# Part of the first expert moved into the first layer's steps, and second-layer rounds of seven chunks instead of eight

## The chip, the cores and the metric

The kernel runs on one core of one Trainium2 chip. The metric is the device time of one execution in microseconds (us). Three executions of the kernel before took 1352.67, 1353.41 and 1355.34 us; the median is 1353.41 us.

## The reference

Two transformer layers over x of shape (8, 512, 128). In each layer attention and feed-forward part read the same normalized input, and both are added to x.

```python
x = L0_attn_encodings                      # (8, 512, 128)
xn = _layernorm(x)                         # eps 1e-5
x = x + _L0_attn_ref(xn, ...) + _L0_ffn_ref(xn, ...)
xn = _layernorm(x)
x = x + _L1_attn_ref(xn, ...) + _L1_ffn_ref(xn, ...)
# attention in both layers: 16 heads of 8, causal softmax over 512 keys
# layer 0 feed-forward: block-quantized linear 128->512, gelu, block-quantized linear 512->128
def expert_step(acc, w):                   # layer 1 feed-forward: all 8 experts for all rows
    wg, wu, wd = w                         # (128,512) (128,512) (512,128)
    h = jax.nn.silu(x @ wg) * (x @ wu)
    return (acc + h @ wd, None)
```

## The kernel before, in words

There are three parts in a row, each a block of its own with a barrier behind it: `layer0`, `attend_moe` (the second layer) and `finish`. Every engine's program is written out in a fixed order; engines meet only at semaphores. No scheduler decides anything.

**First layer.** Attention goes by quads: four heads of one batch, 32 quads in all. One step g of `layer0` computes the row maxima of quad g+1 (scores, six units S0 to S5), the exponentials of half of quad g-1 and half of quad g (transposed scores, units T), the product with the values for quad g-1 (PV), and the feed-forward part of one 128-row tile of layer 0 (q = g-1). u = g mod 4 says which of the batch-wise jobs a step also holds: projections, transposes and the late copies of a batch. Steps run from -7 to 32. The order on TensorE in a step is: scores_and_keys 0, a batch job, fillers 1, scores_and_keys 1, a batch job, fillers 2, scores_and_keys 2, fillers 3, scores_and_keys 3, fillers 4, scores_and_keys 4, PV, scores_and_keys 5, and the end of the step. A filler (`keep_warm`, one 128x128 by 128x512 matmul into `pv_bank`, whose result nobody reads) only occupies TensorE; the table FILLERS says how many stand at each of the four places: 8, 14, 11 and 9 in steps with u = 0, 1, 2, 3.

Matmul results of the first layer live in three pairs of PSUM banks that are used in turn. `units_in_order` lists every unit in program order; unit number i uses pair i mod 3, and `begin` makes TensorE wait until unit i-3 has been read out (`read_out` names the semaphore). So whichever engine reads unit i-3 late holds up unit i, and everything behind it on TensorE.

VectorE reads the score units (`maxima_of`), and between unit 1 and unit 2 it computes the quantization scales of the feed-forward tile (`magic_tile`: a reduce of 512 columns and two small instructions).

**Second layer.** `attend_moe` interleaves attention with the experts. One chunk is 128 of the 512 hidden columns of one expert for one batch: TensorE does `gate_up` (6 matmuls of 512 columns, since every operand is a high and a low part and three products are needed), ScalarE tanh, VectorE `silu` and `product`, ScalarE `hi`, GpSimd `lo`, and TensorE three chunks later `down` (3 matmuls). Every fourth chunk VectorE adds the result to `acc`. There are 8 experts x 8 batches x 4 = 256 chunks, 8 in each of 32 quads. Score units stand in chunks 0 to 5 of a quad, key units in chunks 1 to 6, the transposed maxima (`maxima_rows`, which wait for GpSimd's `rest_of_maxima`) in chunk 7. `LATE` names what is left over from the first layer or is due in a quad (the projections of batches 6 and 7, the attention's share of a batch).

**Hand-over.** The first layer's last step (32) holds only keys, PV and one tile; behind them VectorE takes the statistics of batch 6 and GpSimd normalizes it, and then the second block starts.

## Time and profile before

| | |
|---|---|
| time, median of three | 1353.41 us |
| the profiled execution | 1358.98 us, of which 1357.2 us are the span of the trace |
| mean granted TensorE clock | 0.975 of 2.4 GHz |
| TensorE matmul / weight load busy | 1289.3 us (95%) / 773.8 us (57%) |
| VectorE / ScalarE / GpSimd busy | 980.6 (72%) / 824.3 (61%) / 744.0 us (55%) |
| fillers (L148) | 402 matmuls |
| steps 10 to 29 of the first layer | 182.5 to 475.3 us |
| second layer | 516.6 to about 1333 us |

An engine's busy time counts an instruction from its start to its end; matmuls overlap, so that their pace is read from the distance of two starts. "Idle before" gives an engine's wait and the instruction whose end released it. In rows, L134 are scores, L141 keys (transposed scores), L148 fillers, L159 PV, L950 the mask, L702 and L169 the row maxima, L1562 to L1564 gate and up, L1573 to L1575 down, L1522 the transposed maxima.

### The profile page before, as it was taken

Reading aid. Unit: us, or ns where it says so; the run is one execution under the profiler, and the core shown is the slowest. Engines: PE = TensorE matmul, PEld = TensorE weight load, DVE = VectorE, ACT = ScalarE, POOL = GpSimd, SP = SyncE. Lnnn points to the kernel's source line nnn. Section 1 sums busy time; section 2 is a strip of 40 time slices with the busy share of each in tenths; the row PEclk is TensorE's granted clock in tenths of the full one; section 3 lists DMA queues with packets and bytes.
Section 4 is the critical chain, followed back from the end, with each engine's and each line's share of the span. In section 5 each row is a group of like instructions: output and inputs, shape, how many; then the busy total and the mean of one; then the engine's idle time right before and its main releaser. Section 6 shows DMA issues by size and latency. Waiting matters only on the chain. (4 is left out here: it accounts for less than half of the span.)

```text
span 1357.2 us, 23492 instructions
## 1 busy us (share of the span) xinstructions
PE 1289.3 (95%) x8320; PEld 773.8 (57%) x8328; DVE 980.6 (72%) x2338; ACT 824.3 (61%) x1235; POOL 744.0 (55%) x890
## 2 busy tenths in 40 slices
PE   7899999999999987999999999999999999999996
PEld 5444545554454444656666666666666666666664
DVE  4676777777776666777777777777787788787764
ACT  2456676666765654666566666566566566566561
POOL 6154465655655444665655655655655655655551
PEclk9899999999998897999999999999999999999998
DMA  6222233324433230111211211111111110101002
GB/s 189 67 86 79 88 116 104 123 93 138 128 102 110 72 104 28 42 43 61 66 43 52 73 44 37 42 43 38 42 44 37 41 51 31 42 28 30 18 16 86
DMA packets 57682, 90.93 MB, mean 67 GB/s; under 512 B 12087, under 2 KB 23356, under 8 KB 57566
## 3 DMA queue, kind: packets, MB, share of 16 engines
q1 hardware_dynamic: 56414, 88.91, 21.0%
q8 instruction: 67, 1.10, 0.3%
q10 hardware_dynamic: 1152, 0.52, 0.2%
q14 instruction: 49, 0.40, 0.1%
HBM read 43.75 MB, written 44.53 MB: 65 GB/s over the span
## 5 line engine op out<-in xcount | busy, mean ns | idle before, releaser
L1262 POOL TENSOR_TENSOR a_h_lo<-a_h,a_h_hi 128x512 fp32r<-128x512 f32 x256 | 328.7, 1284 | 139.1 <-ACT a_h_hi L1341 135.8
L193 POOL TENSOR_SCALAR_AFFINE_SELECT E<-E 128x256 f32<-128x256 f32 (+1 forms) x384 | 194.6, 509 | 346.4 <-ACT E L1349 199.4
L702 DVE TENSOR_REDUCE mx<-bank_pair 128x2 f32<-128x1024 f32 (+3 forms) x264 | 209.5, 818 | 117.5 <-PE bank_pair L950 116.2
L1422 DVE SCALAR_TENSOR_TENSOR a_h<-a_h,bank_pair 128x512 f32<-128x512 f32 x256 | 175.5, 686 | 164.1 <-ACT a_h L1337 164.0
L1349 ACT ACTIVATE E<-bank_pair 128x1024 f32<-128x1024 f32 (+1 forms) x192 | 169.6, 883 | 105.2 <-PE bank_pair L141 105.0
L169 DVE CUSTOM_DVE_ANT_0 bank_pair<-bank_pair,mask 128x512 f32<-128x512 f32 x496 | 230.3, 516 | 0.0
L1341 ACT ACTIVATE a_h_hi<-a_h 128x512 fp32r<-128x512 f32 x256 | 161.6, 631 | 110.8 <-DVE a_h L1428 110.8
L134 PE MATMUL bank_pair<-st 24*128 24x512 f32 (+3 forms) x1024 | 201.6, 390 | 21.0 <-DVE mx L169 8.4
L790 ACT ACTIVATE E<-bank_pair 128x1024 f32<-128x1024 f32 (+1 forms) x192 | 168.3, 878 | 69.7 <-PE bank_pair L141 68.1
L1337 ACT ACTIVATE a_h<-bank_pair 128x512 f32<-128x512 f32 x256 | 151.3, 591 | 77.7 <-PE bank_pair L1564 75.4
L1428 DVE TENSOR_TENSOR a_h<-a_h,bank 128x512 f32<-128x512 f32 x256 | 175.9, 687 | 26.7
L141 PE MATMUL bank_pair<-st 26*128 26x512 f32 (+3 forms) x1024 | 185.2, 392 | 2.0 <-DVE mx L702 1.4
L134 PEld LDWEIGHTS bank_pair<-st 24*128 24x128 f32 x1024 | 99.0, 185 | 115.4 <-issue 72.3
L148 PE MATMUL bank<-identr 128*128 128x512 f32 x402 | 139.5, 461 | 2.0 <-POOL identb L492 2.0
L141 PEld LDWEIGHTS bank_pair<-st 26*128 26x128 f32 x1024 | 88.4, 184 | 69.1 <-issue 55.4
L159 PE MATMUL bank<-E,V 128*9 128x512 f32 (+3 forms) x1024 | 86.2, 456 | 3.5 <-POOL E L193 3.5
L148 PEld LDWEIGHTS bank<-identr 128*128 128x128 f32 x402 | 73.9, 206 | 20.0 <-issue 10.1
L159 PE MATMUL bank_pair<-E,V 128*9 128x512 f32 (+3 forms) x1024 | 80.7, 434 | 0.0
L169 DVE DVE_READ_ACCUMULATOR2_ANT mx<- 128x1 f32 x496 | 69.6, 140 | 0.0
L950 PE MATMUL bank_pair<-mask,identb 128*128 128x128 bf16 (+1 forms) x396 | 65.4, 248 | 0.0
L1573 PE MATMUL bank<-a_h_hi,a_w_hi 128*128 128x512 f32 x128 | 63.7, 498 | 1.6 <-POOL a_h_lo L1262 1.6
L1573 PE MATMUL bank<-a_h_hi,w_hi 128*128 128x512 f32 x128 | 64.2, 501 | 0.0
(203 smaller groups left out, 2294.7 us busy)
## 6 DMA issues: line engine op xcount, KB each, us to landing
st<-stack_d SPq DMA_DIRECT2D x256, 96.0 KB
o_d<-O SPq DMA_DIRECT2D x64, 256.0 KB, 2.1
stack_d<-l_q_k_hi SPq DMA_DIRECT2D x56, 256.0 KB, 3.2
stack_d<-l_q_k_lo SPq DMA_DIRECT2D x28, 256.0 KB, 3.4
st<-ms SPq DMA_DIRECT2D x128, 8.0 KB
wst<-wg_in SPq DMA_DIRECT2D x8, 256.0 KB, 3.2
wst<-wu_in SPq DMA_DIRECT2D x8, 256.0 KB, 3.1
wst<-wd_in SPq DMA_DIRECT2D x8, 256.0 KB, 3.6
```

The source lines that it names most:

```text
L134: return nc.tensor.matmul(bank[:, col:col + w], st[rows, 0, bass.ts(t, P)], st[rows, 1, 0:w], start=first, stop=last)
L141: return nc.tensor.matmul(bank[:, col:col + w], st[rows, 1, bass.ts(kb, P)], st[rows, 0, N - w:N], start=True, stop=True)
L148: nc.tensor.matmul(bank[:, :], identr[:, :], columns, start=True, stop=True)
L159: ins = nc.tensor.matmul(pv_bank[VW * c:VW * c + HD + 1, N - w:N], V[:, v:v + HD + 1], E[:, (PLANES * g + j) % slots, at:at + w], start=kb ...
L169: ins = nc.vector.tensor_tensor_reduce(part, part, mask[:, N - w:N], 1.0, NEG, ALU.add, ALU.max, mx[:, g % 2, NT - 1 - kb, PLANES * r + j: ...
L193: return nc.gpsimd.affine_select(out=part, in_=part, compare_op=ALU.is_ge, fill=0.0, base=0, pattern=pattern, channel_multiplier=-1)
L702: ins = nc.vector.tensor_reduce(out, pair[:, :, col:col + width(kb)], AX.X, ALU.max)
L790: nc.scalar.activation(E[:, pair % SLOTS_E, at_col:at_col + HALVES * w].rearrange("p (r c) -> p r c", r=HALVES), pair_of("T", g, n)[:, :, ...
L1262: nc.gpsimd.tensor_tensor(h_lo[:, q % RH, :], h[:, q % RH, :], h_hi[:, q % RH, :].bitcast(F32), ALU.subtract).then_inc(h_lo_ready, 1)
L1349: nc.scalar.activation(E[:, pair % SLOTS_E, at_col:at_col + HALVES * w].rearrange("p (r c) -> p r c", r=HALVES), T_banks[:, :, 0:w], ACT.E ...
L1422: nc.vector.scalar_tensor_tensor(hq, hq, 1.0, g_bank[:, :], ALU.add, ALU.mult).then_inc(silu_ready, 1)
L1428: nc.vector.tensor_tensor(hq, hq, u_bank[:, :], ALU.mult).then_inc(h_ready, 1)
```

## The change

- The first 20 chunks of expert 0 (batches 0 to 4) are computed in steps 10 to 29 of the first layer, one chunk e = g - 10 a step. In each of them stand three groups of three matmuls: `gate` behind filler place 1, into `pv_bank`; `down` of the chunk before (e-1), unit D, ahead of scores_and_keys 2; `up`, unit U, ahead of scores_and_keys 3. D and U take their turn in the three bank pairs.
- In these steps EARLY_FILLERS replaces FILLERS: 2, 7, 2 and 2 fillers for u = 0 to 3.
- ScalarE gets `tanh` (ahead of exp 4 of quad g-1) and `high` (behind exp 0 of quad g); VectorE `silu` and `add_down` behind `magic_tile` and ahead of the maxima of unit 2, and `product` behind them; GpSimd `low` behind the first causal of quad g. `add_down` adds four chunks into `acc_early` and is what frees unit D.
- Expert 0 is loaded at step 4 and split at steps 6 to 8 (before: loaded at 22, split at 24 to 28); expert 1 is loaded at step 31.
- The second layer has 236 chunks. Quads 0 to 11 keep 8 chunks, quads 12 to 31 have 7. `PASSES` gives the order of (expert, batch). In a quad of seven, key unit 5, the transposed maxima and what follows them share the last chunk, and `rest_of_maxima` stands in chunk 5.
- `outputs(g-1)`, the copy of PV's result, moves from chunk 3 to the last chunk of the quad, ahead of `hi`; the store of it moves to the end of SyncE's round. A late unit of attention comes one quad later.
- Layer end (step 32): GpSimd's last causal goes ahead of the tile's shift, ten fillers stand ahead of the last PV, VectorE's statistics of batch 6 stand earlier, and the normalization of batch 6 moves into the second layer's quad 0 (GpSimd, chunk 3).
- `bv` is one row instead of four, `at` is multiplied in place, and `st_rows` shares its buffer with `h`.

The first place is VectorE in step 12 (u = 0) of the first layer, from maxima of unit 1 on. In rows `bank_pair` is a unit, L702 or L761 its maxima, l_gelu the tile. Before:

```order
L702 TENSOR_REDUCE mx<-bank_pair 128x2 x2
L612 TENSOR_REDUCE l_amax<-l_gelu 128x16
L614 TENSOR_SCALAR l_amax<-l_amax 128x16
L616 TENSOR_SCALAR l_magic<-l_amax 128x16
L702 TENSOR_REDUCE mx<-bank_pair 128x2 x2
L619 TENSOR_TENSOR l_quant<-l_shifted,l_magic 128x512
L702 TENSOR_REDUCE mx<-bank_pair 128x2 x3
```

Now (L776 silu, L790 add_down, L781 product):

```order
L761 TENSOR_REDUCE mx<-bank_pair 128x2 x2
L671 TENSOR_REDUCE l_amax<-l_gelu 128x16
L673 TENSOR_SCALAR l_amax<-l_amax 128x16
L675 TENSOR_SCALAR l_magic<-l_amax 128x16
L776 SCALAR_TENSOR_TENSOR l_h<-l_h,bank 128x512
L790 SCALAR_TENSOR_TENSOR acc_early<-bank_pair,acc_early 128x512
L761 TENSOR_REDUCE mx<-bank_pair 128x2
L781 TENSOR_TENSOR l_h<-l_h,bank_pair 128x512
L761 TENSOR_REDUCE mx<-bank_pair 128x2
L678 TENSOR_TENSOR l_quant<-l_shifted,l_magic 128x512
L761 TENSOR_REDUCE mx<-bank_pair 128x2 x3
```

Two instructions now stand between the tile's scales and the maxima of unit 2, and a third behind these.

The second place is TensorE in the same step, from the end of scores_and_keys 1 to fillers 4. Before:

```order
L148 MATMUL bank<-identr 128x512 x2
L141 MATMUL bank_pair<-st 128x256 x2
L134 MATMUL bank_pair<-st 128x256 x2
L950 MATMUL bank_pair<-mask,identb 128x128 x2
L148 MATMUL bank<-identr 128x512 x2
L141 MATMUL bank_pair<-st 128x512 x2
L134 MATMUL bank_pair<-st 128x512 x2
L950 MATMUL bank_pair<-mask,identb 128x128 x2
L148 MATMUL bank<-identr 128x512 x2
```

Now, from unit D on (L1070 to L1072 are down and then up, L170 scores, L177 keys, L184 fillers):

```order
L1070 MATMUL bank_pair<-l_h_hi,w_hi 128x512
L1071 MATMUL bank_pair<-l_h_hi,w_lo 128x512
L1072 MATMUL bank_pair<-l_h_lo,w_hi 128x512
L177 MATMUL bank_pair<-st 128x256 x2
L170 MATMUL bank_pair<-st 128x256 x2
L1049 MATMUL bank_pair<-mask,identb 128x128 x2
L1070 MATMUL bank_pair<-xT_hi,w_hi 128x512
L1071 MATMUL bank_pair<-xT_hi,w_lo 128x512
L1072 MATMUL bank_pair<-xT_lo,w_hi 128x512
L177 MATMUL bank_pair<-st 128x512 x2
L170 MATMUL bank_pair<-st 128x512 x2
L1049 MATMUL bank_pair<-mask,identb 128x128 x2
```

Fillers 2 and 3 are gone, and the matmuls of D and of U stand in their places; fillers 4, behind the last row, stay.

The third place is TensorE at the end of a second-layer quad: the last key unit, down, gate_up and the transposed maxima. Before:

```order
L141 MATMUL bank_pair<-st 128x256 x2
L1573 MATMUL bank<-a_h_hi,a_w_hi 128x512
L1574 MATMUL bank<-a_h_hi,a_w_lo 128x512
L1575 MATMUL bank<-a_h_lo,a_w_hi 128x512
L1562 MATMUL bank_pair<-xT_hi,a_w_hi 128x512
L1563 MATMUL bank_pair<-xT_hi,a_w_lo 128x512
L1564 MATMUL bank_pair<-xT_lo,a_w_hi 128x512
L1562 MATMUL bank<-xT_hi,a_w_hi 128x512
L1563 MATMUL bank<-xT_hi,a_w_lo 128x512
L1564 MATMUL bank<-xT_lo,a_w_hi 128x512
L1522 MATMUL bank_pair<-identr,nm 8x128 x4
```

Now, in a quad of seven chunks (L1653 are the transposed maxima, L177 the last key unit, L1706 on down):

```order
L1693 MATMUL bank_pair<-xT_hi,a_w_hi 128x512
L1694 MATMUL bank_pair<-xT_hi,a_w_lo 128x512
L1695 MATMUL bank_pair<-xT_lo,a_w_hi 128x512
L1693 MATMUL bank<-xT_hi,a_w_hi 128x512
L1694 MATMUL bank<-xT_hi,a_w_lo 128x512
L1695 MATMUL bank<-xT_lo,a_w_hi 128x512
L1653 MATMUL bank_pair<-identr,nm 8x128 x4
L177 MATMUL bank_pair<-st 128x256 x2
L1706 MATMUL bank<-a_h_hi,a_w_hi 128x512
L1707 MATMUL bank<-a_h_hi,a_w_lo 128x512
L1708 MATMUL bank<-a_h_lo,a_w_hi 128x512
```

The last key unit stood one whole chunk ahead of the transposed maxima, and now follows them.

The diff, cut to its core:

```diff
-SPLIT_AT = (24, 26, 28)
+SPLIT_AT = (6, 7, 8)
+EARLY, EARLY_STEP = 5, 10
+EARLY_CHUNKS = EARLY * NC
+EARLY_FILLERS = ((0, 0, 0, 2), (6, 0, 0, 1), (0, 0, 0, 2), (0, 0, 0, 2))
+CHUNKS_OF = [8] * 12 + [7] * 20
+PASSES = [(0, 5)] + [(1, b) for b in range(5)] + [(0, 6), (0, 7)] + [(1, b) for b in range(5, B)] + [(x, b) for x in range(2, EXPERTS) for b in range(B)]
...
 # units_in_order
+        put(("D", g - EARLY_STEP - 1, 0), 0 <= g - EARLY_STEP - 1 < EARLY_CHUNKS)
         scores_and_keys(2)
         put(("X", 0, b + 2), u == 2 and 0 <= b + 2 < B)
+        put(("U", g - EARLY_STEP, 0), 0 <= g - EARLY_STEP < EARLY_CHUNKS)
         scores_and_keys(3)
...
 # read_out
+            return {"F": (gelu_ready, NT * i + 2), "U": (early_h, i + 1), "D": (early_added, i + 1),
...
 # GpSimd, first layer
+            def low(e):
+                pool.wait_ge(early_hi, e + 1)
+                nc.gpsimd.tensor_tensor(h_lo, h, h_hi.bitcast(F32), ALU.subtract).then_inc(early_lo, 1)
...
-                if q is not None:
+                if q is not None and g < QUADS:
                     shift_tile(q)
                 if in_range(g - 1):
                     causal(g - 1, 5)
+                if g == QUADS:
+                    shift_tile(q)
...
-                if u == 0 and ok(y2):
+                if u == 0 and ok(y2) and g < QUADS:
                     normalize(1, y2)
...
 # VectorE, first layer
+            def silu(e):
+                dve.wait_ge(early_tanh, e + 1)
+                nc.vector.scalar_tensor_tensor(h, h, 1.0, pv_bank[:, :], ALU.add, ALU.mult).then_inc(early_silu, 1)
+            def product(e):
+                dve.wait_ge(early_up, e + 1)
+                dve.wait_ge(early_silu, e + 1)
+                nc.vector.tensor_tensor(h, h, bank_of("U", e, 0), ALU.mult).then_inc(early_h, 1)
+            def add_down(e):
+                dve.wait_ge(early_down, e + 1)
+                ...
+                    nc.vector.scalar_tensor_tensor(a, bank_of("D", e, 0), 0.5, a, ALU.mult, ALU.add).then_inc(early_added, 1)
...
                 if q is not None:
                     magic_tile(q)
+                if g == QUADS:
+                    statistics(1, y2)
                 if u == 3 and ok(a):
                     unshift_x(a)
+                if early(g - EARLY_STEP):
+                    silu(g - EARLY_STEP)
+                if early(g - EARLY_STEP - 1):
+                    add_down(g - EARLY_STEP - 1)
                 if S:
                     maxima_of(g + 1, 2)
...
 # TensorE, first layer
+            def down(e):
+                pe.wait_ge(early_lo, e + 1)
+                begin("D", e, 0)
+                thrice(bank_of("D", e, 0), 2, e, h_hi, h_lo, True, True).then_inc(early_down, 1)
...
+                if g == QUADS:
+                    pe.wait_ge(O_copied, g - 1)
+                    keep_warm(nc, pv_bank, identr, 10)
+                if early(g - EARLY_STEP):
+                    up(g - EARLY_STEP)
                 fill(g, 3)
                 scores_and_keys(g, 3)
...
 # second layer, GpSimd and ScalarE
+            for g, c, last, q in chunks_in_order():
+                if c == CHUNKS_OF[g] - 2 and g + 1 < QUADS:
+                    rest_of_maxima(g + 1)
+                if 0 < c <= UNITS_A_QUAD:
+                    causal(g, c - 1)
+                lo(q)
...
+                tanh(q)
+                if last and g + 1 < QUADS:
+                    copy_mrow(g + 1)
+                if 0 < c <= UNITS_A_QUAD:
+                    exp(g, c - 1)
+                if last and g > 0:
+                    outputs(g - 1)
+                hi(q)
```

## Rows read from the trace of the kernel before

**Rows 1.** Windows: us, busy us (x) per engine, clock, DMA share, GB/s; stages.

```profile
182.50:240.00 57.50, 54.80 (x453) 28.61 (x454) 42.38 (x85) 38.95 (x56) 33.98 (x45) 1.00 0.37 113
851.30:1102.70 251.40, 248.37 (x1425) 158.97 (x1425) 196.97 (x518) 158.89 (x246) 148.69 (x163) 1.00 0.14 43
```

**Rows 2.** Timeline of step 12: start us, us, engine, line, op [idle before].

```profile
213.99 1.29 DVE L702 TENSOR_REDUCE mx<-bank_pair 128x2 f32<-128x768 f32 x2 [0.54 <-PE bank_pair L950]
...
216.34 1.81 DVE L702 TENSOR_REDUCE mx<-bank_pair 128x2 f32<-128x512 f32 x2
...
215.14 0.71 PE L148 MATMUL bank<-identr 128*128 128x512 f32 x2
...
215.78 0.50 PE L141 MATMUL bank_pair<-st 26*128 26x512 f32 x2
```

**Rows 3.** Timeline of steps 13 (two rows), 14 (three) and 15 (two).

```profile
229.20 1.29 DVE L702 TENSOR_REDUCE mx<-bank_pair 128x2 f32<-128x768 f32 x2 [2.46 <-PE bank_pair L950]
...
231.68 0.49 PE L141 MATMUL bank_pair<-st 26*128 26x512 f32 x2
...
243.10 1.29 DVE L702 TENSOR_REDUCE mx<-bank_pair 128x2 f32<-128x768 f32 x2 [0.92 <-PE bank_pair L950]
...
246.76 0.68 DVE L702 TENSOR_REDUCE mx<-bank_pair 128x2 f32<-128x512 f32 x1
...
247.50 0.50 PE L134 MATMUL bank_pair<-st 24*128 24x512 f32 x2 [0.54 <-DVE mx L702]
...
257.51 1.29 DVE L702 TENSOR_REDUCE mx<-bank_pair 128x2 f32<-128x768 f32 x2 [0.92 <-PE bank_pair L950]
...
260.16 0.50 PE L141 MATMUL bank_pair<-st 26*128 26x512 f32 x2
```

**Rows 4.** Timeline, VectorE in the second layer, two instructions back to back.

```profile
1088.78 0.69 DVE L1428 TENSOR_TENSOR a_h<-a_h,bank 128x512 f32<-128x512 f32 x1
1089.40 0.69 DVE L1437 SCALAR_TENSOR_TENSOR acc<-bank,acc 128x512 f32<-128x512 f32 x1
```

**Rows 5.** Timeline, last two chunks of a second-layer quad.

```profile
1099.22 0.17 DVE L1417 TENSOR_REDUCE nm<-mx 128x16 fp32r<-128x16 f32 x1
...
1099.76 0.39 PE L141 MATMUL bank_pair<-st 26*128 26x256 f32 x2
...
1100.07 0.50 PE L1573 MATMUL bank<-a_h_hi,a_w_hi 128*128 128x512 f32 x1
...
1102.27 0.40 PE L1522 MATMUL bank_pair<-identr,nm 128*8 128x128 f32 x4
```

**Rows 6.** Timeline, end of the first layer to the second layer's first matmul.

```profile
503.57 1.05 POOL L509 TENSOR_TENSOR l_shifted<-l_gelu,l_magic 128x512 f32<-128x512 f32 x1
...
505.05 3.11 PE L159 MATMUL bank<-E,V 128*9 128x512 f32 x16 [3.52 <-POOL E L193]
...
510.08 0.29 DVE L686 TENSOR_TENSOR xs<-bank,xs 128x128 f32<-128x128 f32 x1 [4.54 <-PE bank L1065]
...
513.11 3.13 POOL L504 TENSOR_SCALAR xn<-xs,mv,rstd 128x128 f32<-128x128 f32 x4
...
516.59 0.77 PE L1562 MATMUL bank_pair<-xT_hi,w_hi 128*128 128x512 f32 x1 [6.55 <-PEq L291]
```

**Rows 7.** Windows: the second layer's first 5 us.

```profile
516.00:521.00 5.00, 4.41 (x10) 2.87 (x11) 2.02 (x5) 1.21 (x2) 0.24 (x1) 0.50 0.49 146
```

**Rows 8.** Timeline, two TensorE waits of 2 us in the first layer.

```profile
73.88 0.66 PE L993 MATMUL bank_pair<-ident,l_xn 128*128 128x128 f32 x4 [2.15 <-POOL l_xn L504]
...
130.93 0.66 PE L993 MATMUL bank_pair<-ident,l_xn 128*128 128x128 f32 x4 [2.08 <-POOL l_xn L504]
```

**Rows 9.** Windows: behind either wait of rows 8, and one step at a fallen clock.

```profile
73.00:78.00 5.00, 4.12 (x20) 2.80 (x21) 1.30 (x3) 1.62 (x3) 3.18 (x6) 0.66 0.16 50
130.00:135.00 5.00, 4.07 (x35) 2.58 (x39) 2.90 (x6) 2.49 (x4) 3.66 (x7) 1.00 0.35 99
282.91:298.48 15.57, 14.61 (x108) 8.14 (x106) 10.65 (x23) 10.07 (x16) 9.56 (x13) 0.90 0.20 63
```

More of the change, by code:

```diff
@@ L236, in __init__, with acc_of @@
         self.xn, self.xnT = sb("xn1", [P, NT, D]), sb("xnT1", [P, N])
+def acc_of(acc, b):
+    return acc[0][:, bass.ts(b, N)] if b < EARLY else acc[1][:, bass.ts(b - EARLY, N)]
 def load_expert(sp, wst, experts, x, done):
@@ L587, in _ @@
                         causal(g, n)
-                if u == 0 and ok(y2):
+                        if n == 0 and early(g - EARLY_STEP):
+                            low(g - EARLY_STEP)
+                if u == 0 and ok(y2) and g < QUADS:
                     normalize(1, y2)
@@ L871, in _ @@
                     parts(0, a, 0)
+                if early(g - EARLY_STEP):
+                    tanh(g - EARLY_STEP)
                 if in_range(g - 1):
@@ L1090, in _ @@
                 fill(g, 1)
+                if early(g - EARLY_STEP):
+                    gate(g - EARLY_STEP)
                 scores_and_keys(g, 1)
@@ L1097, in _ @@
                     keys(0, a)
+                if early(g - EARLY_STEP - 1):
+                    down(g - EARLY_STEP - 1)
                 fill(g, 2)
@@ L1577, in down @@
                     ins.then_inc(acc_ready, 1)
-            for i in range(STEPS):
-                g, odd = i // PLANES, i % PLANES
-                more, back = g + 1 < QUADS, not odd and g > 0
-                for n in range(NC):
-                    gate_up(i, n)
-                    if odd and n == 3 and more:
-                        maxima_rows(g + 1)
-                        if g in LATE:
-                            late_unit(*LATE[g])
-                    c = NC * odd + n
-                    scores_and_keys(g, c if c < UNITS_A_QUAD else None, c - 1 if 0 < c <= UNITS_A_QUAD else None)
-                    if back and n == 0:
-                        PV(g - 1, 0)
-                        PV(g - 1, 1)
-                    if back and n == 1:
-                        PV(g - 1, 2)
-                        PV(g - 1, 3)
-                    if NC * i + n >= LAG:
-                        down(NC * i + n - LAG)
-            for q in range(NC * STEPS - LAG, NC * STEPS):
+            for g, c, last, q in chunks_in_order():
+                more, back = g + 1 < QUADS, g > 0
+                gate_up(q)
+                if last and more:
+                    maxima_rows(g + 1)
+                    if g in LATE:
+                        late_unit(*LATE[g])
+                scores_and_keys(g, c if c < UNITS_A_QUAD else None, c - 1 if 0 < c <= UNITS_A_QUAD else None)
+                if back and c == 0:
+                    PV(g - 1, 0)
+                    PV(g - 1, 1)
+                if back and c == 1:
+                    PV(g - 1, 2)
+                    PV(g - 1, 3)
+                if q >= LAG:
+                    down(q - LAG)
+            for q in range(NC * len(PASSES) - LAG, NC * len(PASSES)):
                 down(q)
@@ L1657, in sums @@
                     o = sum_banks[b % 4][:, bass.ts(t, D)]
-                    ins = nc.tensor.matmul(o, acc[:, bass.ds(b * N + t * P, P)], ident[:, :], start=True, stop=b < last)
+                    ins = nc.tensor.matmul(o, acc_of(acc, b)[:, bass.ts(t, P)], ident[:, :], start=True, stop=b < last)
                     if b == last:
```

279 lines of the change are left out of this document (162 added, 117 removed).

## The prediction

> **What bounds the kernel now.** I read the windows by stage first, then the timeline of single steps on TensorE and VectorE side by side, then the waits. The windows say that TensorE is busy nearly all the time in both layers: 54.8 of 57.5 us over four first-layer steps, 248.4 of 251.4 us in the second layer [rows 1]. In the first layer part of that is fillers, 8 to 14 matmuls a step. VectorE has 42.4 of 57.5 us there, and 197.0 of 251.4 in the second layer. So in the second layer real work on TensorE sets the time, and a chunk taken away is time gained. In the first layer the question is not how much room TensorE has, since fillers can go, but whether the new work waits for something that fillers never waited for. The timeline answers that.
>
> **Second layer, 20 chunks fewer.** In the last two chunks of a quad, down of one chunk starts at 1100.07 and the transposed maxima behind the next gate_up at 1102.27: nine matmuls in 2.20 us, 0.244 each [rows 5]. Chunk 7 holds nothing else that is paid by the quad, so 20 x 2.20 = 44.0 us go. What is late next: VectorE's top maxima are read at 1099.22 and end 0.17 later; with GpSimd's small instruction behind them they are ready near 1099.7, and gate_up of chunk 6 ends where the key unit starts, at 1099.76 [rows 5]. So the transposed maxima would just not wait. But with seven chunks a quad, VectorE's add into acc (0.62 from start to start, [rows 4]) moves through the quad, and in most quads it falls on a chunk with maxima, on which the next score unit or the transposed maxima wait. One add each for ten of the 20 quads is 6 us; nothing and twice that are the bounds. The output copy moves ahead of hi on ScalarE, with the store and the load of the maxima queued behind it on SyncE; down is three chunks behind, and the loaded maxima are wanted only by the first key unit of the next quad, so I take nothing for it; a load that comes late would cost up to 1 us a quad. Together -38 us (-44 to -24).
>
> **First layer, 20 steps with early work.** By instructions this is cheap. Per batch there are 36 matmuls more and 29 fillers fewer (42 against 13), 7 x 0.244 = 1.7 us, 8.5 us for five batches. But unit U takes the bank pair that unit D had, so up waits until add_down has read D. On VectorE add_down stands behind maxima 1, the tile's scales and silu, and none of these can start before scores 1 are there. In step 12 maxima 1 starts at 213.99 and the instruction behind the scales at 216.34: 2.35 us. Silu and add_down are instructions of 512 columns with a PSUM operand, 0.62 us each from start to start [rows 4], 0.1 for the semaphore (estimate), and then up, three matmuls: two fillers take 0.64 (215.14 to 215.78, [rows 2]), three 0.88. From maxima 1 to the start of scores_and_keys 3 that is 2.35 + 1.24 + 0.10 + 0.88 = 4.57 us. Before it is 215.78 - 213.99 = 1.79. The step grows by 2.8, and by another 0.24 because gate has one matmul more than the two fillers of place 1: 3.0 us (u = 0). The waits stand in front of work that is all TensorE's own, so nothing later gives them back: scores and keys 4 follow exp 0, which follows key unit 0.
>
> The other steps in the same way [rows 3]. u = 1: before 231.68 - 229.20 = 2.48, now 4.57: 2.1 us (gate and fillers 1 together are one matmul fewer there, which the transposes behind them wait for anyway). u = 2: the scales take longer, 243.10 to 246.76 is 3.66; add_down ends at 248.1, four transposes and up bring scores 3 to 249.35, against 247.50, where it already waited for VectorE: 1.85 + 0.24 = 2.1 us. u = 3: another instruction of 512 columns (unshift_x) stands ahead of silu, so 4.57 + 0.62 = 5.2 against 260.16 - 257.51 = 2.65: 2.5 us, the matmul of gate and one filler fewer at place 4 cancelling. Sum 9.7 a batch, 48.5 for five; the first early step has no unit D, -2.0. So +46.5 us. The bounds: 8.5 where the wait is hidden, and 60 where every step also pays 0.6 us for tanh ahead of exp 4, on which D waits. ScalarE's table need not change for tanh beside exp, since the second layer already runs both.
>
> **Clock.** These are waits of 1 to 2.7 us in each of 19 steps. Two waits of 2.15 and 2.08 us stand in the trace [rows 8]: behind the first the granted clock is 0.66 over 5 us, behind the second it stays at 1.00 [rows 9]; the fillers that stood there go. A step with a fall took 15.57 us [rows 9] against 57.50 / 4 = 14.4, 1.2 us more. Ten such falls are 12 us; against them stand this one and, as an estimate, two more like it that steps 10 to 29 have already, 4 us. +8 us; the bounds are -4 (no fall at all) and +34 (2 us in each of 19 steps, less the 4).
>
> **Hand-over.** The first layer's last instruction is GpSimd's normalization, from 513.11 for 3.13 us, and TensorE starts at 516.59, 0.35 behind it [rows 6]. The normalization moves; the last is then VectorE's add, 510.08 + 0.29. The tile's shift (1.05) no longer stands ahead of the last causal, and PV, 3.11 us at half clock, should take half of that behind ten fillers that fill its wait of 3.52 [rows 6]: 510.37 - 1.05 - 1.5 + 0.35 = 508.2, so -8.4 us. The second layer's first 5 us ran at clock 0.50 [rows 7]; at full clock they are worth 2.5. The normalization (4.2 us with its power) and three splits of 1.28 are then on GpSimd in quad 0, which costs 1. Sum -10 (-6 to -12).
>
> **Sum.** -38 + 46.5 + 8 - 10 = +6.5 us. The profiled execution took 1358.98 us with a span of 1357.2; it becomes 1365.5. The median of the runs shown is 5.6 below the profiled one, so 1353.4 + 6.5 = 1360 us.
>
> The other steps (6 to 8 with the splits, 30 with its unit D) I put at nothing: ScalarE and GpSimd have a third of the step free in them, and D costs 0.9 us once.
>
> **Rivals.**
> - Waits paid, nothing else. The chain D to U costs its 46.5 us, but the clock stays up, and VectorE's add finds room in the shorter quads: 1353.4 - 44 + 46.5 - 10 = 1346 us. For it: the second wait of rows 8 leaves no trace on the clock. Against it: the first one does.
> - The early work hides. Place: up in the first layer. If add_down ended before TensorE is through scores and keys 2, the early work would cost its 7 matmuls a batch alone: 1353.4 + 8.5 - 38 - 10 = 1314 us, the side away from my forecast. It decides 1.4 us behind the start of maxima 1, where up could start (215.14 - 213.99 before, and a matmul of 0.24 more, [rows 2]); add_down ends at 2.35 + 1.24 = 3.6. For it speaks the first layer's VectorE, idle for 15 of 57.5 us; against it, that this idle time lies before maxima 1, where VectorE waits for scores (0.54 to 2.46 us, [rows 2, 3]). The Trainium skill (Perfetto Trace Analysis, Identifying the Most-Contended Engine) says to judge TensorE by the busy share of its weight loads and not by that of its matmuls, and under Optimization Strategy that regimes with different bounds may gain by interleaving. Here the loads take 28.6 of 57.5 us in the first layer and 159.0 of 251.4 in the second [rows 1], which by that rule is room in the first, and the time would be that of this rival.
> - The clock falls in most early steps: +34 in place of +8 would be 1386; with some of it behind waits, 1380 us. For it: TensorE loses the fillers just where it now waits. Against it: the new matmuls are as long as fillers were.
> - The change doesn't do what it says. The order of the instructions shows D, U and 20 rounds of seven in their places, so I give it nothing.
>
> **Chances.** Forecast 0.48, with a range of its own of 1352 to 1369; waits paid alone 0.21; hidden 0.12; clock mostly low 0.19. For 8 in 10 the range takes in the first of the rivals and the last, and leaves the hidden case out: 1336 to 1384 us. A measurement of this kernel tells 0.2% (2.7 us) from no change. Faster are the two rivals below and a little of the forecast: 0.36. Within 0.2%: 0.10. Slower: 0.54.
>
> **What would show it.** Steps 10 to 29 take about 292.8 us before; with me 340 to 355, with the hidden case 300. Up (unit U) has an idle time of about 2 us in u = 0, 1 in u = 1 and 1 to 2 in u = 3, and the transposes ahead of it 2 to 3 in u = 2, all ended by VectorE's add into acc_early. The second layer's quads of seven take 22.9 us where VectorE keeps up, 23.2 with its adds. The second layer's first matmul comes 8 to 9 us sooner after the last transposed maxima of the first. If up never waits for VectorE, my largest term is wrong, and if the quads of seven are above 24 us, something other than TensorE sets them.

## The result: slower, 1386.96 us

The kernel after takes 1386.96 us (1381.84 to 1389.24, four runs), the kernel before 1353.04 us in the runs beside it: the ratio is 1.0244, 95% interval 1.0208 to 1.028. The forecast was 1360 us with 1336 to 1384 as its range, so the direction was right and the size was not: 34 us slower, where 6.5 were expected. The profiled execution took 1389.24 us, with a span of 1387.5. The profiled pair differs by less, 30.3 us of span, since the profiled execution of the kernel before was 5.6 us over its median.

The profile after, first its page: part 1 (busy us, share, instructions) and two lines of part 2 (40 slices; `PEclk` is the granted clock in tenths).

```profile
PE 1296.5 (93%) x8185; PEld 765.8 (55%) x8193; DVE 982.2 (71%) x2353; ACT 818.6 (59%) x1235; POOL 740.9 (53%) x890
...
PEclk9899988988887897999999999999999999999999
```

TensorE is busy a little longer than before (1289.3 us) though it has 135 matmuls fewer (8320 before). The second line says why: in the slices that hold steps 10 to 29 the clock is 0.7 to 0.9. The windows say it by stage: three of six pieces of steps 10 to 29, the end of the first layer, and the second layer's rounds 1 to 11 and then 19 rounds of seven. Columns as in [rows 1], which the first row answers.

```profile
181.90:240.00 58.10, 51.90 (x355) 25.73 (x357) 36.82 (x70) 32.79 (x50) 29.20 (x37) 0.82 0.31 95
...
300.00:360.00 60.00, 52.80 (x352) 25.30 (x354) 38.88 (x80) 34.97 (x52) 33.83 (x43) 0.84 0.27 81
...
420.00:486.00 66.00, 59.85 (x405) 27.65 (x405) 39.29 (x77) 35.50 (x53) 31.30 (x41) 0.80 0.22 68
...
558.00:586.00 28.00, 27.19 (x232) 15.19 (x231) 21.17 (x40) 17.26 (x25) 12.14 (x18) 1.00 0.47 144
615.30:896.60 281.30, 277.97 (x1597) 180.44 (x1596) 217.10 (x577) 182.56 (x286) 173.31 (x189) 1.00 0.16 51
896.60:1337.20 440.60, 429.44 (x2521) 274.19 (x2521) 346.83 (x941) 275.70 (x427) 245.19 (x280) 1.00 0.13 40
```

Before, the first stage had a clock of 1.00 [rows 1]. Cutting the record into windows of 2 us shows each fall: in steps 10 to 29 there are 18 falls to half clock (1.2 of 2.4 GHz) with 125.9 us spent there, against 3 and 20.4 before. A step with a fall takes 17.5 to 20.5 us; the only two without one took 16.0 (step 14) and 14.8 (step 26). In the second layer the clock is up (1.00 in both windows above).

Stage by stage, from the copies of the transposed maxima (one a step or round):

| | before | after | difference | forecast |
|---|---|---|---|---|
| steps 10 to 29 | 292.8 | 376.5 | +83.7 | +54.5 |
| last copy of layer 1 to first of layer 2 | 40.9 | 30.9 | -10.0 | -10 |
| rounds 1 to 11 | 284.3 | 281.3 | -3.0 | } -38 |
| 19 rounds from the twelfth on | 477.2 | 440.6 | -36.7 | } |

The twentieth round of seven lies behind the last copy. From there to the last down it is 27.4 us before and 26.0 after, and to the end of the span 54.2 and 50.3.

Two of the three places came out near the forecast, and so did the waits in the third. The timeline of TensorE after in steps 12 to 15 (start us, us, engine, line, operation, idle before and releaser) has L1070 as the first matmul of up and L1121 as the transposes ahead of it in u = 2:

```profile
225.59 0.50 PE L1070 MATMUL bank_pair<-xT_hi,w_hi 128*128 128x512 f32 x1 [1.74 <-DVE acc_early L790]
...
246.30 0.50 PE L1070 MATMUL bank_pair<-xT_hi,w_hi 128*128 128x512 f32 x1 [0.89 <-DVE acc_early L790]
...
266.02 0.63 PE L1121 MATMUL bank_pair<-ident,l_xn 128*128 128x128 f32 x4 [1.93 <-DVE acc_early L790]
...
281.79 0.54 PE L1070 MATMUL bank_pair<-xT_hi,w_hi 128*128 128x512 f32 x1 [1.29 <-DVE acc_early L787]
```

The forecast named about 2, 1, 2 to 3 and 1 to 2 us (u = 0, 1, 2, 3), all ended by VectorE's add into `acc_early`, as they are. The groups of steps 10 to 29 on TensorE (count, busy, mean ns, idle before by releaser) give the sum for up, 20.8 us in 20 steps:

```profile
L1070 PE MATMUL bank_pair<-xT_hi,w_hi 128*128 128x512 f32 x20 | 12.6, 630 | 20.8 <-DVE acc_early L790 13.9 <-DVE acc_early L787 6.9
```

The hand-over after, in the timeline of three engines, answers [rows 6]:

```profile
585.05 0.86 DVE L707 BATCH_NORM_STATS2 stats<-xs 128x6 f32<-128x128 f32 x4
...
587.80 1.05 POOL L562 TENSOR_TENSOR l_shifted<-l_gelu,l_magic 128x512 f32<-128x512 f32 x1
...
587.88 1.69 PE L195 MATMUL bank<-E,V 128*9 128x512 f32 x16
...
592.25 0.47 PE L1693 MATMUL bank_pair<-xT_hi,w_hi 128*128 128x512 f32 x1 [0.66 <-PEq L334]
```

PV no longer waits and runs at full clock (1.69 us for 3.11), and the second layer's first matmul waits 0.66 us, not 6.55. It comes 8.2 us sooner behind the last transposed maxima of the first layer, where 8 to 9 were forecast. Two more windows answer [rows 9] and [rows 7], a stretch of 16 us with falls (0.90 in the step there) and 5 us from the second layer's first matmul on (0.50 there):

```profile
281.00:297.00 16.00, 14.94 (x111) 7.81 (x111) 9.10 (x16) 6.83 (x10) 6.80 (x9) 0.79 0.31 93
592.00:597.00 5.00, 4.48 (x20) 2.68 (x20) 2.69 (x6) 2.23 (x4) 0.94 (x1) 1.00 0.54 162
```

### The profile page after: what moved, and what is told of

Read it like the earlier page. It is cut to its first block and busy times, and to the rows that moved or that the text cites. A ratio compares the mean times of both kernels' runs of the same rounds, so it can differ in the third digit from the quotient of the medians.

```text
span 1387.5 us, 23344 instructions
## 1 busy us (share of the span) xinstructions
PE 1296.5 (93%) x8185; PEld 765.8 (55%) x8193; DVE 982.2 (71%) x2353; ACT 818.6 (59%) x1235; POOL 740.9 (53%) x890
## 5 line engine op out<-in xcount | busy, mean ns | idle before, releaser
L1398 POOL TENSOR_TENSOR a_h_lo<-a_h,a_h_hi 128x512 fp32r<-128x512 f32 x236 | 303.1, 1284 | 105.3 <-ACT a_h_hi L1477 101.2
L761 DVE TENSOR_REDUCE mx<-bank_pair 128x2 f32<-128x1024 f32 (+3 forms) x264 | 209.9, 819 | 154.5 <-PE bank_pair L1049 154.2
L1552 DVE SCALAR_TENSOR_TENSOR a_h<-a_h,bank_pair 128x512 f32<-128x512 f32 x236 | 161.8, 686 | 134.5 <-ACT a_h L1473 133.9
L170 PE MATMUL bank_pair<-st 24*128 24x512 f32 (+3 forms) x1024 | 210.3, 407 | 19.1 <-DVE mx L205 6.1
L177 PE MATMUL bank_pair<-st 26*128 26x512 f32 (+3 forms) x1024 | 191.7, 408 | 4.8 <-DVE mx L761 3.1
L1477 ACT ACTIVATE a_h_hi<-a_h 128x512 fp32r<-128x512 f32 x236 | 148.6, 630 | 72.9 <-DVE a_h L1558 72.8
L1558 DVE TENSOR_TENSOR a_h<-a_h,bank 128x512 f32<-128x512 f32 x236 | 162.1, 687 | 26.4 <-DVE a_h L1552 2.3
L1473 ACT ACTIVATE a_h<-bank_pair 128x512 f32<-128x512 f32 x236 | 140.1, 594 | 68.3 <-PE bank_pair L1695 66.3
L170 PEld LDWEIGHTS bank_pair<-st 24*128 24x128 f32 x1024 | 104.0, 195 | 112.7 <-issue 77.3
L177 PEld LDWEIGHTS bank_pair<-st 26*128 26x128 f32 x1024 | 92.9, 193 | 74.3 <-issue 59.1
L195 PE MATMUL bank<-E,V 128*9 128x512 f32 (+3 forms) x1024 | 102.8, 527 | 0.0
L184 PE MATMUL bank<-identr 128*128 128x512 f32 x267 | 95.4, 478 | 2.0 <-POOL identb L545 2.0
L1706 PE MATMUL bank<-a_h_hi,a_w_hi 128*128 128x512 f32 x128 | 64.1, 501 | 1.3 <-POOL a_h_lo L1398 1.3
L935 ACT ACTIVATE l_hqT<-bank 128x512 bf16<-128x512 bf16 x32 | 19.1, 597 | 76.9 <-PE bank L1146 76.9
L184 PEld LDWEIGHTS bank<-identr 128*128 128x128 f32 x267 | 52.3, 217 | 12.1 <-issue 3.7
```

The costliest lines, as they stand in the source:

```text
L170: return nc.tensor.matmul(bank[:, col:col + w], st[rows, 0, bass.ts(t, P)], st[rows, 1, 0:w], start=first, stop=last)
L177: return nc.tensor.matmul(bank[:, col:col + w], st[rows, 1, bass.ts(kb, P)], st[rows, 0, N - w:N], start=True, stop=True)
L195: ins = nc.tensor.matmul(pv_bank[VW * c:VW * c + HD + 1, N - w:N], V[:, v:v + HD + 1], E[:, (PLANES * g + j) % slots, at:at + w], start=kb ...
L761: ins = nc.vector.tensor_reduce(out, pair[:, :, col:col + width(kb)], AX.X, ALU.max)
L1398: nc.gpsimd.tensor_tensor(h_lo[:, q % RH, :], h[:, q % RH, :], h_hi[:, q % RH, :].bitcast(F32), ALU.subtract).then_inc(h_lo_ready, 1)
L1477: nc.scalar.activation(h_hi[:, q % RH, :], h[:, q % RH, :], ACT.Copy).then_inc(h_hi_ready, 1)
```

## Experiments

In all of them "steps" are steps 10 to 29 of the first layer. Each was timed in turns with the kernel before.

| run | edit | time, us | ratio to before (95%) | steps, us | falls, us at half clock |
|---|---|---|---|---|---|
| 1 | scales behind the experts' work | 1354.99 | 1.0014 (0.9992 to 1.0035) | 341.0 | 8, 27.0 |
| 2 | fillers in the wait | 1348.07 | 0.9965 (0.9942 to 0.9988) | 334.5 | 2, 10.1 |
| 3 | kernel before, few fillers | 1376.63 | 1.0165 (1.0131 to 1.0199) | 314.2 | 19, 94.8 |
| 4 | fillers ahead of the wait | 1392.70 | 1.0283 (1.0222 to 1.0343) | 377.1 | 16, 88.4 |
| 5 | 1, and the last causal first | 1338.32 | 0.9896 (0.9869 to 0.9923) | 320.7 | 1, 3.4 |
| 6 | 5, and more fillers | 1344.48 | 0.994 (0.9916 to 0.9964) | 328.5 | 1, 3.4 |
| 7 | after, add to acc later | 1371.09 | 1.0145 (1.0119 to 1.0172) | 362.5 | 16, 92.0 |
| 8 | after, normalization back | 1388.07 | 1.0248 (1.0204 to 1.0292) | 366.3 | 16, 98.4 |
| 9 | 5 and 7 | 1321.37 | 0.9766 (0.9737 to 0.9795) | 322.3 | 1, 10.2 |
| 10 | 9 without fillers in the steps | 1336.88 | 0.9882 (0.9848 to 0.9915) | 328.9 | 11, 44.1 |
| 11 | 9, product behind the scales | **1315.38** | 0.972 (0.969 to 0.9749) | 314.8 | 2, 6.6 |
| 12 | kernel before, add to acc later | 1347.73 | 0.9959 (0.9944 to 0.9973) | 286.5 | 1, 3.4 |

The two right columns are of the one profiled execution each.

### 1. The wait taken away: VectorE's order

```diff
+                if early(g - EARLY_STEP - 1):
+                    add_down(g - EARLY_STEP - 1)
+                if early(g - EARLY_STEP):
+                    silu(g - EARLY_STEP)
+                    maxima_of(g + 1, 2)
+                    product(g - EARLY_STEP)
                 if q is not None:
                     magic_tile(q)
```

(the old places of the four calls go for these steps)

> The changed kernel, but in the early steps VectorE does add_down, silu, maxima 2 and product directly behind maxima 1, and the tile's scales behind them. Theory A (add_down's place behind the scales makes up wait, and the wait brings the clock down): the wait of up drops from 0.9 to 1.9 us to about 0.5 us or less, most falls of the clock in steps 10 to 29 go, the steps take about 300 to 315 us in place of 376, and the time is 1310 to 1325 us. Theory B (the early work itself, or the fillers taken out, brings the clock down, the wait costs only itself): the waits go, 25 us, the falls stay, about 1360 us. Theory C (the wait moves: the scales come late, and the turning of the tile waits for them instead): about 1380 us.

Measured: 341.0 us for the steps, 35.4 less than after, 8 falls. Up no longer waits for VectorE (0.2 us in all, for 20.8), but a new wait of PV stands in every step, 23.7 us in all, and GpSimd's timeline beside TensorE's names its cause:

```profile
221.67 1.05 POOL L562 TENSOR_TENSOR l_shifted<-l_gelu,l_magic 128x512 f32<-128x512 f32 x1 [3.46 <-DVE l_magic L675]
...
223.14 1.69 PE L195 MATMUL bank<-E,V 128*9 128x512 f32 x16 [1.11 <-POOL E L229]
```

The shift of the tile waits for the scales, which are late now, and the last causal, for which PV waits, is queued behind the shift. The wait went from one engine's queue to another's. No theory had this whole: ten falls went, as theory A said, the wait moved, as theory C said, and the time lies between A's 1325 and B's 1360.

### 2. The wait kept, but filled

```diff
                 scores_and_keys(g, 2)
+                if early(g - EARLY_STEP) and early(g - EARLY_STEP - 1):
+                    keep_warm(nc, pair_of("D", g - EARLY_STEP - 1, 0)[:, 1, :], identr, (7, 4, 8, 5)[u])
```

> The changed kernel with fillers in the wait itself: 7, 4, 8 and 5 fillers (u = 0 to 3) behind scores_and_keys 2, into the unused bank of the pair of unit D. Up starts when it did. Theory A (TensorE standing still in front of up brings the clock down): no or few falls in steps 10 to 29, and the time is lower by what the falls cost, 18 falls of 1.5 to 3 us: 1335 to 1360 us. Theory B (the clock falls for the early steps' other work, wherever the fillers stand): falls stay, 1387 us or more.

Measured: steps of 17.49, 16.77, 16.02 and 16.64 us in u = 0 to 3, 334.5 in all. This is the kernel after with its chain from D to U untouched, and matmuls that nobody reads in the wait. The windows of its steps (as above):

```profile
181.15:515.67 334.52, 316.29 (x2398) 169.75 (x2398) 235.41 (x461) 210.96 (x312) 188.74 (x242) 0.98 0.30 93
```

More matmuls (2398, against 2288 in the pieces of after), and 42 us less, as theory A said. So of the 83.7 us, 42.0 go with 16 of the 18 falls, and 41.7 stay for the chain.

Steps without a fall show that the fillers add nothing of their own. Step 14 of after took 16.00 us, and in runs 7 and 8, whose steps have the code of after, steps without a fall took 16.77 (u = 1) and 16.63 (u = 3). The kernel before takes 14.45, 14.66, 14.36 and 14.06 us in steps 12 to 15, where it has no fall. So the chain costs 3.0, 2.1, 1.7 and 2.6 us, where the prediction had 3.0, 2.1, 2.1 and 2.5.

### 3 and 4. Is it the wait, or the missing fillers?

Run 3 is the kernel before with only the table changed (2, 7, 2 and 2 fillers in steps 10 to 29); run 4 is the kernel after with more fillers at place 1, ahead of the wait:

```diff
-EARLY_FILLERS = ((0, 0, 0, 2), (6, 0, 0, 1), (0, 0, 0, 2), (0, 0, 0, 2))
+EARLY_FILLERS = ((5, 0, 0, 2), (11, 0, 0, 1), (5, 0, 0, 2), (5, 0, 0, 2))
```

> The kernel before, with the changed kernel's number of fillers (2, 7, 2, 2 in place of 8, 14, 11, 9) in steps 10 to 29, and no early work. Theory A (a wait of 1 to 2 us is needed for a fall): no more falls than before, and as fillers are only work, steps 10 to 29 get shorter by up to 29 x 0.244 = 7 us a batch: 1318 to 1335 us. Theory B (fewer fillers are enough for the clock to fall): falls in most steps, which cost as much or more than the fillers did: 1350 to 1375 us.

> The changed kernel with five fillers more in each early step, but at place 1, ahead of gate, so that the wait of up stays as long as it is. Theory A (the wait itself brings the clock down): falls stay, and the fillers cost 5 x 0.24 us a step more: 1400 to 1412 us. Theory B (the count of matmuls in a step decides): the falls go, 1345 to 1375 us.

Measured, the windows of the steps in run 3 and the first lines of its waits of TensorE there (us in total, times, longest), and then one TensorE row of run 4:

```profile
182.41:496.62 314.21, 285.60 (x2109) 131.93 (x2109) 204.80 (x402) 191.73 (x274) 168.26 (x225) 0.85 0.34 103
```

```profile
PE bank_pair L135 <- ACT E L791: 9.8, 12, 1.6
PE bank_pair L135 <- DVE mx L703: 5.9, 5, 1.5
```

```profile
223.38 0.66 PE L1070 MATMUL bank_pair<-xT_hi,w_hi 128*128 128x512 f32 x1 [1.75 <-DVE acc_early L790]
```

Few fillers alone bring the clock to 0.85, with none of the experts' work and no wait over 1.6 us. The same two waits take 3.5 and 2.7 us in the kernel before: they stay, and grow, when the fillers in them go. That is theory B of run 3, with a time just over its range. In run 4 five more fillers a step ahead of the wait leave the wait at 1.75 us (step 12) and the steps at 377.1 us. The falls stay (16 for 18), as theory A said, but time at half clock goes from 125.9 to 88.4 us, and the 1392.70 us lie under A's 1400: what these fillers give back in clock they cost in their own length. So the number of matmuls does not decide (2398 in the steps of run 2, 2386 in those of run 4); a filler pays where TensorE would otherwise stand still, whoever it waits for.

### 5 and 6. The moved wait taken away too

```diff
-                if q is not None and g < QUADS:
+                if q is not None and g < QUADS and not early(g - EARLY_STEP):
                     shift_tile(q)
                 if in_range(g - 1):
                     causal(g - 1, 5)
-                if g == QUADS:
+                if g == QUADS or early(g - EARLY_STEP):
                     shift_tile(q)
```

Run 6 adds fillers to it, 14 a batch: 2, 1, 2 and 2 at place 1, and 2, 2, 1 and 2 behind scores_and_keys 2 (its expectation speaks of 2 or 3 more a step; it is 3 or 4).

> The kernel after, with VectorE's order of the first experiment, and with GpSimd's last causal multiplication of a step ahead of the shift of the tile in steps 10 to 29 (the shift waits for VectorE's scales, which come late in that order). Fillers stay at 2, 7, 2 and 2. Theory A (the 1.1 to 1.5 us for which PV waits for GpSimd in every early step is the shift's place in GpSimd's queue): the wait goes, 20 x 1.2 = 24 us of it leave the 341 us of steps 10 to 29, but with so few fillers TensorE's clock still falls now and then, as it did in the kernel before with few fillers (19 falls): steps 10 to 29 at 318 to 328 us, time 1332 to 1342 us. Theory B (the wait hides another one behind it, of the tile's quantized value or of the bank pairs): PV waits less and the next unit or transpose waits about 1 us more, steps at 335 to 341 us, time 1349 to 1355 us. If the clock needs fillers whatever the waits are: over 12 falls and more than 50 us at half clock, time 1350 us or more.

> The experiment before this one (scales late, last causal first), with fillers in steps 10 to 29 at 4, 9, 3 and 4 and a last one or two where the table has them: 2, 7, 2 and 2 ahead of unit 1, and 2, 2, 1 and 2 behind scores_and_keys 2. A filler is about 0.24 us of TensorE, so 20 steps get 20 x 2 or 3 x 0.24 = 10 to 15 us of work more. Theory A (with the waits gone, what is left is the clock, and fillers cure it): no more than 3 falls, steps 10 to 29 at 315 to 325 us and within 6 us of the kernel without these fillers, time 1330 to 1340 us, faster than both kernels. Theory B (the clock has already recovered with the waits gone): fillers only add their own time, 10 to 15 us over the kernel without them.

Measured: in run 5 the steps take 320.7 us with one fall, the last causal is through before PV, and PV does not wait:

```profile
223.89 0.42 POOL L229 TENSOR_SCALAR_AFFINE_SELECT E<-E 128x256 f32<-128x256 f32 x1 [0.52 <-ACT E L875]
226.83 1.05 POOL L562 TENSOR_TENSOR l_shifted<-l_gelu,l_magic 128x512 f32<-128x512 f32 x1 [2.52 <-DVE l_magic L675]
```

Theory A had the time and the steps right, and its doubt about the clock wrong: the same 13 fillers a batch that did not hold the clock in run 3 hold it here, beside the experts' matmuls. In run 6 fillers have next to nothing left to cure (one fall in each run) and cost 7.8 us in the steps, half their own time (70 x 0.24 = 17); the other half falls into waits. The medians differ by 6.2 us, between the two theories of run 6.

### 7 and 12. The addition ahead of the maxima

```diff
-                if q % NC == 2 and q > NC:
-                    add_acc(q // NC - 1)
                 if more and c < UNITS_A_QUAD:
                     unit(g + 1, c)
                 if more and c == UNITS_A_QUAD - 1:
                     tops(g + 1)
+                if q % NC == 2 and q > NC:
+                    add_acc(q // NC - 1)
```

Run 12 is the same edit in the kernel before.

> The kernel after; in a chunk of the second layer that adds the result of down to acc, VectorE's addition stands behind the row maxima of the chunk and not ahead of them. Rounds of seven chunks take 21.9 to 24.7 us with a mean of 23.19, 0.29 us more than seven chunks of eight of the rounds before. Theory A (the step of the prediction: the addition of 0.6 us stands ahead of the maxima for which the last keys of a round wait, in the rounds where it falls into the last chunks): the mean of the 19 rounds goes to 22.9 us, 4 to 6 us less in all. Theory B (the longer rounds are longer since they hold one addition or one attention share more, wherever it stands): no difference of more than 1.5 us in the sum of the 19 rounds. Early steps as in the kernel after (375 to 378 us), so that the total is 1381 to 1387 us by A and 1387 by B.

> The kernel before, with VectorE's addition to acc behind the row maxima in the chunks that hold both. In rounds of eight chunks the addition falls into chunks 2 and 6, and only chunk 2 has maxima. Theory A (the addition delays the bank pair of the next unit also in rounds of eight): a round takes 0.2 to 0.5 us less, 6 to 15 us in all, so that time is 1338 to 1347 us and the gain of the seven-chunk rounds is smaller against this kernel. Theory B (in rounds of eight there is slack, and the addition costs only where it falls into the last chunks): within 2 us of the kernel before.

Measured: the 19 rounds take 428.0 us for 440.6, rounds 1 to 11 279.3 for 281.3: 14.6 us less. The longest round of seven (24.63 to 24.92 us, every fourth) becomes 22.94 to 23.38. TensorE and VectorE in one of them, in the kernel after:

```profile
976.25 0.35 PE L170 MATMUL bank_pair<-st 24*128 24x256 f32 x1 [0.26 <-DVE mx L205]
976.92 0.38 PE L170 MATMUL bank_pair<-st 24*128 24x256 f32 x1 [0.32 <-DVE mx L205]
...
986.79 0.69 DVE L1569 SCALAR_TENSOR_TENSOR acc_early<-bank,acc_early 128x512 f32<-128x512 f32 x1
...
988.29 0.17 DVE L1547 TENSOR_REDUCE nm<-mx 128x16 fp32r<-128x16 f32 x1
...
988.82 0.41 PE L1653 MATMUL bank_pair<-identr,nm 128*8 128x128 f32 x4 [0.66 <-POOL nm L1413]
```

and in run 7:

```profile
968.79 0.17 DVE L1547 TENSOR_REDUCE nm<-mx 128x16 fp32r<-128x16 f32 x1
968.88 0.69 DVE L1569 SCALAR_TENSOR_TENSOR acc_early<-bank,acc_early 128x512 f32<-128x512 f32 x1
...
969.32 0.41 PE L1653 MATMUL bank_pair<-identr,nm 128*8 128x128 f32 x4
```

The maxima no longer stand behind the add, and TensorE has none of the three waits. In rounds of eight (run 12) the same edit is worth 3.8 us in both parts (284.3 to 283.0 and 477.2 to 474.9), so 10.8 of the 14.6 us are a cost of the seven-chunk rounds, where the forecast had 6. Theory A of run 7 had the place right and the size too low (12.6 us in the 19 rounds, not 4 to 6); run 12 lies between its two. Run 7's total fell by 15.9 us; its steps varied too (362.5 us with the same code in them as after, in the fastest of its four executions).

### 8. The normalization put back

```diff
-                if u == 0 and ok(y2) and g < QUADS:
+                if u == 0 and ok(y2):
                     normalize(1, y2)
```

(and its call in the second layer, with the waits on it, goes)

> The kernel after, with the normalization of batch 6 back at the end of the first layer (before: behind its last step, after: in the second layer's first round), all else of the layer's end as in the kernel after. The hand-over, from the last first-layer copy of transposed scores to the first of the second layer, is 30.9 us in the kernel after and 40.9 in the kernel before. Theory A (the gain of 10 us is that normalization, which was the last thing ahead of the barrier): hand-over 39 to 41 us, time up by 8 to 10 us to 1395 us. Theory B (most of it is the rest: fillers ahead of the last product with the values, VectorE's statistics and GpSimd's order): hand-over 32 to 36 us, time up by 1 to 5 us.

Measured: 31.88 us, 0.9 more than after, with a total 1.1 us higher. The next round takes 25.25 us for 24.64, 0.6 more. This is theory B, whose range for the hand-over began at 32. With the statistics early, the normalization runs beside the end of TensorE's work, and TensorE waits 1.84 us for the second layer:

```profile
582.04 3.13 POOL L557 TENSOR_SCALAR xn<-xs,mv,rstd 128x128 f32<-128x128 f32 x4
...
585.53 0.47 PE L1691 MATMUL bank_pair<-xT_hi,w_hi 128*128 128x512 f32 x1 [1.84 <-PEq L334]
```

So nine of the ten us are there without the move. How they divide among the statistics, the order on GpSimd and the ten fillers was not tried, nor what the move would give without them.

### 9 to 11. Both orders together, and the fillers once more

Run 9 joins 5 and 7. Run 10 sets EARLY_FILLERS to zero everywhere; run 11 moves one call:

```diff
                     maxima_of(g + 1, 2)
-                    product(g - EARLY_STEP)
                 if q is not None:
                     magic_tile(q)
+                if early(g - EARLY_STEP):
+                    product(g - EARLY_STEP)
```

> The kernel after with three orders changed: VectorE's scales of the tile late, GpSimd's last causal ahead of the tile's shift (both as in the experiment that took 1338 us) and in the second layer VectorE's addition to acc behind the row maxima. The two savings stand in different parts of the program (steps 10 to 29: 320.7 us against 376.5; second layer 14.6 us less), so the theory that each is a wait of its own place expects their sum: 1338 - 14.6 = 1324 us, steps 10 to 29 at 318 to 326 us, the 19 rounds of seven at 428 us. The rival, that a time this much varies with where the clock's falls happen to lie, expects steps 10 to 29 at 330 us or more, with more than 6 falls, and 1333 us or more.

> The kernel of the run before this one in the list, without any filler in steps 10 to 29 (before: 13 a batch, 65 in all, of 0.24 us: 15.5 us of TensorE's time). Theory A (TensorE's share of real work is what holds the clock, and the experts' nine matmuls a step suffice once nobody waits long): no more than 4 falls, and the time falls by the fillers that stood on TensorE's path, 8 to 15 us, to 1309 to 1316 us. Theory B (fillers stand where TensorE would wait, and hold the clock): more than 8 falls and more than 30 us at half clock in steps 10 to 29, time 1324 us or more.

> The kernel of the first run of this list with VectorE's scales of the tile (0.68 + 0.17 + 0.17 us) ahead of product and not behind it in steps 10 to 29. The transposes of l_quant wait 0.9 us for VectorE in two of four steps. Theory A (that wait is the scales' late place): it goes, 5 x 1.8 = 9 us less, of which some comes back since product, and with it U's bank pair, is 1.1 us later: time 0 to 8 us less than without this change. Theory B (the pair of U is what the next unit waits for): the wait for l_quant goes and one of about 1 us for product stands behind it in most steps, time 0 to 15 us more, and more falls of the clock.

Measured, the steps of runs 9, 10 and 11 in windows:

```profile
182.26:504.60 322.34, 291.93 (x2281) 153.47 (x2286) 246.16 (x461) 210.80 (x312) 191.09 (x242) 0.98 0.31 96
```

```profile
182.47:511.39 328.92, 292.91 (x2216) 147.47 (x2221) 246.46 (x461) 211.19 (x311) 191.75 (x242) 0.93 0.31 94
```

```profile
182.27:497.11 314.84, 285.78 (x2281) 150.41 (x2286) 241.09 (x461) 211.70 (x311) 192.25 (x242) 0.99 0.32 98
```

The savings add up (1321.4 us, forecast 1324). Run 10 has 65 matmuls fewer and is 15.5 us slower: the last 13 fillers a batch still hold the clock, 11 falls without them and 1 with them, so theory B was right there. TensorE's waits for ScalarE's exponentials ahead of a score unit add up to 10.7 us in its steps, against 1.8 in run 9, which has the fillers. Only 6.6 us of the 15.5 stand in the steps of the profiled execution, which at 1330 us of span was the fastest of its four; 3.9 more stand behind the last copy of transposed maxima (54.2 us for 50.3). Run 11 took away most of the transposes' wait for `l_quant` (8.1 us in ten steps of run 9, 1.2 left) and left the next unit waiting for product (9.6 us in 16 steps, 0.3 to 0.9 each):

```profile
220.11 0.44 PE L177 MATMUL bank_pair<-st 26*128 26x384 f32 x2 [0.53 <-DVE l_h L781]
```

The steps are 7.5 us shorter. These two waits do not explain it, since they more than cancel; 6.1 of the 7.5 us are time that counts as busy (291.9 to 285.8 with the same matmuls), and what shortened it stays open. It is the fastest kernel of this study: 1315.38 us, 2.8% under the kernel before and 5.2% under the kernel after.

## Why the prediction was wrong

- **Clock, +8.** This is the step that failed: "Ten such falls are 12 us". There were 18 falls in 20 steps. Run 2 has 16 fewer and takes 42.0 us less in the steps, which is 2.6 us for each and not 1.2. Both factors were off by about two. The price came from one step whose fall had been short (clock 0.90 over it), and it was set against the mean of four kinds of step, 14.4 us, not against its own kind (14.66 in step 13); the falls of after spend 7 us at half clock each. The count came from two waits that stood among fillers [rows 8, 9]. Run 3 shows what the step overlooked: the fillers that the change removes had held the clock, so that it falls even without the new wait. It was the third rival, "the clock falls in most early steps", put at 0.19 with 1380 to 1386 us, and its argument against ("the new matmuls are as long as fillers were") holds only for a TensorE that does not wait (run 5). The bound of +34 for this term was too low too. The credit of 4 us for the falls that were there already was low as well: in run 12, with the same code in these steps, the three steps with a fall before (17, 27 and 29) take 7.3 us less.
- **First layer, the chain from D to U, +46.5.** Right: 9.4 us a batch in steps without a fall, where 9.7 were put, and 41.7 us over all steps of run 2, which is a little low since the kernel before has three falls in them and run 2 two. Only u = 2 was put too high, 2.1 for 1.7 us. The waits stand where they were forecast, within 0.3 us of the named sizes or bounds. The arithmetic from the row of maxima 1 to up was the sound part of the working. "Steps 10 to 29 with me 340 to 355 us" missed by the clock alone (376.5).
- **Second layer, -38.** Near as a sum (-39.7, and 1.4 more in the twentieth round), by luck, since two errors cancelled in it. The addition ahead of the maxima was to cost 6 us more than before and costs 10.8 more (14.6 less 3.8, runs 7 and 12). The chunks were put at 2.20 us each, read from one stretch of TensorE. With the addition behind the maxima in both kernels, the 19 rounds of seven take 46.9 us less (474.9 in run 12, 428.0 in run 7), 2.5 a chunk; an eighth of a round would be 3.1. Rounds 1 to 11, which lose no chunk, give 3.6 us too (283.0 and 279.3); what in them does was not tried. The bound of -24 has room for late loads (20 us) but not for the additions (up to 12) beside them.
- **Hand-over, -10.** Right in size (-10.0), not shown in its reason: the working credited it above all to the normalization that moves away. Run 8 puts it back and loses 0.9 us, so with early statistics the move was hardly needed.
- **Rivals.** "Waits paid, nothing else", 1346 us, is nearly run 2 (1348.07) for the chain and the clock; that the addition finds room in the shorter rounds was wrong. "The early work hides" (1314 us) needed two queues reordered, not one. That run 11 takes 1315.38 us is luck for this number: its steps still take 22.0 us more than before, not 8.5, and 14.6 us come from the addition in the second layer. TensorE's busy time in these steps is 285.8 us against 278.9, and the rest is waits. The Trainium skill (Perfetto Trace Analysis, Identifying the Most-Contended Engine) judges TensorE's room by the busy share of its weight loads. These runs agree that there was a gain to be had, but the kernel after did not have it: the loads' share says nothing of the order in the other engines' queues.
- **The range** ended at 1384, 3 us under the result. It was to hold the clock rival too, and by that rival's own upper number it should have gone past 1386.

## What to carry to other kernels

Before real work replaces fillers, find out what each filler stands in for: a wait for another engine stays when its filler goes, and can then cost the clock (run 3: 24 us). When an instruction is put into an in-order queue, name who waits for everything behind it there; here three small reorderings on VectorE and one on GpSimd, with no work removed, turned 2.4% slower into 2.8% faster. Here the new order on VectorE needed a matching one on GpSimd before it paid (runs 1 and 5).

## What the runs showed of the hardware

- TensorE at clock 0.85 with 285.6 of 314.2 us busy (91%, run 3), and at 0.99 with 290.6 of 320.7 (run 5, 91% too). The busy share of a long stretch does not tell whether the clock holds; a record that counts time at half clock as busy hides it.
- With the same instructions in the steps, executions differ in where the falls come: 376.5, 362.5 and 366.3 us for the steps of after, run 7 and run 8, with 18, 16 and 16 falls. Four executions of one kernel spread over 4.9 to 18.7 us where the steps have 16 falls or more (after and runs 3, 4, 7, 8), and over 3.5 to 6.4 us where they have 11 or fewer (runs 5, 9, 10, 11).
- A fall lasts longer than the waits beside it: beside waits of 0.9 to 1.9 us stand 18 falls with 125.9 us at half clock, 7.0 us each. The two waits of over 2 us in the kernel before [rows 8], one with a fall behind it and one without, told neither how often nor for how long the clock would be down here.
